# Later row groups' preparation two attention steps later in every engine's queue: a graph attention and mixture-of-experts kernel

## The chip, the cores and the metric

The kernel runs on one core of a Trainium2 chip. The metric is the device time of one execution in microseconds. The engines are TensorE (PE; its weight loads are PEld), VectorE (DVE), ScalarE (ACT), GpSimd (POOL) and SyncE (SP), which issues transfers. Each has a queue of its own that it works off in order, and they meet only at semaphores.

## The reference

4096 rows x of 128 features, a sparse 4096 x 4096 adjacency matrix (entries 0 or 1), one attention head, then eight experts of which each row takes two:

```python
h = layernorm(x)
Wh = h @ W_w + W_b
e = leaky_relu((Wh @ a1)[:, None] + (Wh @ a2)[None, :], 0.2)
x = x + softmax(where(adj > 0, e, -9e15), axis=1) @ Wh
g = layernorm(x)
top, idx = top_k(g @ Wg.T + bg, 2)
p = softmax(top)
x = x + sum over the two experts e in idx of p_e * (relu(g @ W1[e].T + b1[e]) @ W2[e].T + b2[e])
```

## The kernel before, in words

**Rows and steps.** Of the 4096 rows, partition p holds rows 32p to 32p + 31; column u of that layout is a source tile of 128 rows (TILES = 32), and four neighbouring tiles are a row group i (GROUPS = 8). The attention runs in five stages over the target rows (8, 8, 8, 6 and 2 tiles wide), each over all 32 source tiles: 160 attention steps n. The change concerns the first stage, steps 0 to 31, where the source rows are prepared as they are needed.

**One attention step.** SP loads the mask as int32, a mask tile for two steps at a time; ACT turns it into bf16 (`edges`, L1321, into G_all); DVE weighs a tile (`weigh`, L948: prob from G_all, a row vector s_bc and the column E_col of this source tile); PE multiplies it with the source rows (`attend`, L1548, acc<-prob,Wh, two multiplications of 512 columns, four records in the trace). prob has six buffers, G_all four. DVE's loop runs four steps ahead of PE's (LB), ACT's mask tiles six (LG), SP's loads twelve (LS).

**Preparing a row group i.** Sums of a row (`stats`, DVE, L867 to L872) give its variance; POOL raises it to -1/2 (`pow_group`, L693 to L701); ACT normalises into Wh (`normalise`, L1286); PE transposes (`transposes`, L1499); ACT copies the result (`keep_hT`, L1295); PE projects it (`project`, L1509, into pj; for groups 2 and 3 `project_s`, L1518, as well); ACT makes two columns of it, w_col and E_col (`keep_E`, L1302 and L1303, and `keep_s`, L1313, for groups 2 and 3); DVE rescales the group's Wh with w_col (`keep_Wh`, L887). Weighing of step 4i waits for E_col of group i, and PE's step 4i for its rescaled Wh. Groups 0 and 1 are prepared ahead of the loop.

**What sets the order.** Each engine has a function `main` that walks n and writes at each n what belongs there; `group_at(n, part)` says which group has its turn in that place, every fourth step:

```python
def group_at(n, part, first=2):
    i, r = divmod(n - part, 4)
    return i + 2 if r == 0 and first <= i + 2 < GROUPS else None
```

**What else stands in these queues.** The experts' first-layer weights are brought in during the stage: ACT issues the loads (`load_expert`, L1337 to L1339), POOL subtracts a row (`shift_weights`, L707), ACT writes the high part (`high_weights`, L1331), DVE the low part (`low_weights`, L1005), for expert 0 at n = 8, 10, 12 and for expert 1 at n = 14, 16, 18, expert 2 at n = 20, 22, 24. At n = 18 DVE writes Wx (L1234, L1235), at n = 20 PE turns it (`gate_weights`, L1694, L1695), at n = 26 DVE makes the gate's terms (L1226 to L1229), and at n = 28 PE needs them (`gate_columns`, L1700). s_bc of the second stage is capped at n = 24 (L933). Behind the first stage, attention steps, sending of rows to their experts and the experts' multiplications are interleaved by counts of the same n.

Of the kernel before, what the change touches and what calls it, by code (L numbers as in the profile page):

```python
# [5 lines left out]
def build(nc, x, adjT, W, Wb, a, WgT, bg, wcat, wlast, b2, out):  # L6
# [119 lines left out]
    with ctx:  # L126
# [319 lines left out]
# [4 lines that stand above are left out]
# [398 lines left out]
        def _(dve):  # L848
# [81 lines left out]
            def group_row(g):  # L930
                dve.wait_ge(s_sbc, (AT[g] + WB[g] + GT - 1) // GT)
                c = c_bc[:, P * AT[g]:P * (AT[g] + WB[g])]
                nc.vector.tensor_scalar(c, c, 1.0, None, ALU.min).then_inc(s_cg, 1)  # L933
# [271 lines left out]
            def main(general):  # L1205
                for n in range(-LB, NS):
# [1 line left out]
                    if m < STEPS and (m or general):  # L1208
                        (weigh_general if general else weigh)(m)
                    if not general:  # L1210
                        i = group_at(n, -7, 4)
                        if i is not None:
                            stats(i)
                        i = 1 if n == -1 else group_at(n, 3)
                        if i is not None:
                            keep_Wh(i, False)
                        if n >= 0 and n % TILES == TILES - 8 and n // TILES + 1 < SG:
                            group_row(n // TILES + 1)
# [42 lines left out]
            with dve.If(fast != 0):  # L1261
                group_row(0)
                weigh(0)
                keep_Wh(0, False)
                stats(3)
                main(False)
            with dve.Else():
                links[0] = before
# [13 lines left out]
        def _(act):  # L1282
# [123 lines left out]
            def main(general):  # L1406
                ahead = LB if general else LG
                for n in range(-ahead, NS):
# [3 lines left out]
                    if m < STEPS and general:  # L1412
                        raise_tile(m)
                    if not general:
                        i = group_at(n, -1)
                        if i is not None:
                            normalise(i)
                        i = group_at(n, 2)
                        if i is not None:
                            keep_hT(i)  # L1420
                        if n == -1:
                            keep_E(1)
                        i = group_at(n, 3)
                        if i is not None:
                            keep_E(i)
                            if i < GT:
                                keep_s(i, general)
                        i = row_at(n)
                        if i is not None:
                            keep_s(i, general)  # L1430
# [59 lines left out]
        def _(pe):  # L1490
# [211 lines left out]
            def main(general):  # L1702
                for n in range(NS):
                    if n == 20:
                        gate_weights()
                    if n == 28:
                        pe.wait_ge(s_xg, 1)
                        gate_columns()
                    if not general:
                        i = group_at(n, 1)  # L1710
                        if i is not None:
                            transposes(i)
                        if n == 1:
                            project(1)
                        i = group_at(n, 3)
                        if i is not None:
                            project(i)
                            if i < GT:
                                project_s(i)
                        i = row_at(n)  # L1720
                        if i is not None:
                            project_s(i, True)
                    if n >= STEPS:
                        tail_beat(TAIL + n - STEPS)
                    if n < STEPS:
                        attend(n)
                    for part in parts_of(n):
                        finish(*part)
# [53 lines left out]
```

## Time and profile before

| | us |
|---|---|
| three runs | 450.41, 452.68, 457.28 (median 452.68) |
| the profiled execution, whole | 449.83 |
| its span on the core | 448.1 |
| PE busy in the span | 396.3 (88%) |
| DVE, ACT, POOL busy | 294.0, 263.9, 200.6 |

The span is the time from the first to the last instruction in the profile; the execution's own time has 1.7 us more around it. Starts in the profile are counted from the start of the span. A row of the timeline merges neighbouring instructions of a kind; its time runs from the first start to the last end, and ends overlap the next start a little, so the step from one row's start to the next is the better measure of pace.

### The profile page before, as it was taken

What the parts mean: (1) busy time and instruction counts of PE and PEld (TensorE: products, weight loads), DVE (VectorE), ACT (ScalarE), POOL (GpSimd) and SP (SyncE); (2) the same over time, 40 slices, a digit from 0 to 9 for tenths busy, and PEclk for the clock granted to TensorE, in tenths of its full rate; (3) what the DMA queues carried; (4) which work ended last, traced back from release to release, by engine and by line L of the source; (5) the groups of instructions that cost most, each with busy time, mean ns of one, the idle gap of its engine ahead of it and who ended that gap; (6) DMA issues with size and microseconds to landing.
All of it is one profiled execution on the core that took longest, in us unless ns stands there. A gap on an engine that the chain in (4) does not pass through costs nothing.

```text
span 448.1 us, 8397 instructions
## 1 busy us (share of the span) xinstructions
PE 396.3 (88%) x2434; PEld 262.8 (59%) x2434; DVE 294.0 (66%) x806; ACT 263.9 (59%) x451; POOL 200.6 (45%) x247
## 2 busy tenths in 40 slices
PE   2799999999999999989999999898789798899960
PEld 2355555354444444434666777686679788888850
DVE  5889879988999796999878831887105800111162
ACT  1688888387677757924679545373346345555630
POOL 3373411100415752066431877766666644444460
PEclk9899999999999999999999999999899979999995
DMA  6999898869698997985879663664656545565784
GB/s 212 362 419 348 324 318 290 369 241 384 266 314 317 337 414 251 324 303 170 302 236 378 214 194 129 215 198 155 215 182 218 186 164 163 174 216 183 240 329 144
DMA packets 45324, 116.46 MB, mean 260 GB/s; under 512 B 7485, under 2 KB 19266, under 8 KB 38614
## 3 DMA queue, kind: packets, MB, share of 16 engines
q1 hardware_dynamic: 37494, 101.07, 63.5%
q0 software_dynamic: 4320, 8.47, 5.6%
q10 hardware_dynamic: 3456, 6.29, 4.4%
q8 instruction: 23, 0.38, 0.4%
q14 instruction: 31, 0.25, 0.2%
HBM read 84.57 MB, written 13.07 MB: 218 GB/s over the span
## 4 chain that ended last, share of the span: by engine, by line
PE 66%; issue 9%; DMA 6%; DVE 6%; ACT 6%; SPq 3%; another core or an unknown queue 2%; POOL 1%; ACTq 0%; POOLq 0%; DVEq 0%
PE acc L1548 36%; PE acc L1650 11%; DVE prob L948 3%; PE hps L1634 3%; PE hps L1632 3%; PE hps L1633 3%; ACT G_all L1321 3%; PE yt L1650 3%; DMA adj<-adjT 3%; PE yt L1593 2%; PE pj L1509 1%; DMA xbuf<-xr,slot 1%; DMA adj<-ybuf 1%; PE pj L1669 1%
## 5 line engine op out<-in xcount | busy, mean ns | idle before, releaser
L1548 PE MATMUL acc<-prob,Wh 128*128 128x512 f32 (+1 forms) x576 | 237.7, 553 | 6.7 <-DVE Wh L887 3.1
L948 DVE SCALAR_TENSOR_TENSOR prob<-s_bc,E_col,G_all 128x1024 f32<-128x1024 f32 (+2 forms) x160 | 172.0, 1105 | 31.8 <-PE acc L1548 20.0
L1548 PEld LDWEIGHTS acc<-prob,Wh 128*128 128x128 f32 x576 | 104.5, 192 | 101.7 <-issue 88.2
L1321 ACT ACTIVATE G_all<-adj 128x2048 bf16<-128x2048 int32 (+1 forms) x67 | 118.9, 1800 | 19.0 <-DVE prob L948 10.3
L799 POOL DMA_INDIRECT ybuf<-wst,dest x71 | 73.0, 1028 | 70.0 <-ACT wst L1404 41.5
L783 POOL DMA_INDIRECT xbuf<-xr,slot x64 | 72.2, 1128 | 56.5 <-DVE slot L1105 19.6
L1650 PE MATMUL acc<-wall,prob 128*128 x368 | 54.1, 289 | 4.5 <-issue 4.5
L1650 PEld LDWEIGHTS acc<-wall,prob 128*128 128x128 f32 x368 | 46.5, 196 | 6.1 <-issue 5.3
L1192 DVE COPY share<-slab 128x1 f32<-128x1 f32 x45 | 6.9, 157 | 62.2 <-DMA slab<-xbuf 41.0
L1394 ACT ACTIVATE prob<-hps 128x512 f32<-128x512 f32 x46 | 28.0, 608 | 31.5 <-PE hps L1634 19.3
L1394 ACT ACTIVATE wst<-hps 128x512 f32<-128x512 f32 x25 | 14.9, 598 | 22.8 <-remote 17.1
L1650 PE MATMUL yt<-wall,wst 128*128 x192 | 27.3, 286 | 0.0
L707 POOL TENSOR_TENSOR wst<-wst,wlb 127x512 f32<-127x512 f32 x8 | 12.0, 1508 | 33.9 <-DMA wlb<-wlast 33.9
L1650 PEld LDWEIGHTS yt<-wall,wst 128*128 128x128 f32 x192 | 23.7, 194 | 4.1 <-issue 2.6
L693 POOL TENSOR_TENSOR scratch<-scratch,mhalf 128x4 f32<-128x4 f32 x8 | 13.4, 1675 | 26.9 <-DVE scratch L872 26.9
L1633 PE MATMUL hps<-prob,s_bc 128*128 128x128 f16 x124 | 23.0, 222 | 1.0 <-issue 1.0
L1632 PE MATMUL hps<-prob,s_bc 128*128 128x128 f16 x124 | 22.9, 222 | 0.8 <-issue 0.8
L1634 PE MATMUL hps<-prob,s_bc 128*128 128x128 f16 x124 | 23.1, 222 | 0.0
L1404 ACT ACTIVATE wst<-acc,share 128x128 f32<-128x128 f32 x45 | 16.6, 372 | 10.8 <-PE acc L1650 6.9
L1593 PE MATMUL yt<-ident,slab 128*128 128x128 f16 x142 | 19.7, 220 | 3.5 <-issue 2.0
L765 POOL TENSOR_TENSOR rstd<-ve,mhalf 128x8 f32<-128x8 f32 x3 | 5.5, 1824 | 34.4 <-DVE ve L1050 34.4
L1389 ACT ACTIVATE prob<-yt 128x256 f16<-128x256 f16 x45 | 17.6, 392 | 5.2 <-PE yt L1593 3.2
(237 smaller groups left out, 543.8 us busy)
## 6 DMA issues: line engine op xcount, KB each, us to landing
adj<-adjT SPq DMA_DIRECT2D x52, 1024.0 KB
adj<-adjT SPq DMA_DIRECT2D x16, 768.0 KB
s_bc<-wall SPq DMA_DIRECT2D x47, 256.0 KB
wlb<-wall SPq DMA_DIRECT2D x24, 256.0 KB
slab<-xbuf SPq DMA_DIRECT2D x71, 65.0 KB
adj<-ybuf SPq DMA_DIRECT2D x6, 512.0 KB
xs<-x SPq DMA_DIRECT2D x8, 256.0 KB, 10.6
wst<-wcat ACTq DMA_DIRECT2D x8, 256.0 KB, 4.6
```

What stands on the lines that cost most here:

```text
L783: nc.gpsimd.indirect_dma_start(xbuf[:, :], bass.IndirectOffsetOnAxis(ap=slot[:, w, b:b + 1].bitcast(u32), axis=0), xr[:, w, b, :], None).t ...
L799: nc.gpsimd.indirect_dma_start(ybuf[:, :], bass.IndirectOffsetOnAxis(ap=dest[:, t:t + 1].bitcast(u32), axis=0), ysb[t % YR][:, :], None, b ...
L948: nc.vector.scalar_tensor_tensor(prob[n % PR][:, 0:w], c_bc[:, P * AT[g]:P * AT[g] + w], E_col[:, u:u + 1], G[m % GR][:, k * w:(k + 1) * w ...
L1321: nc.scalar.activation(G[m % GR][:, 0:w], adj_sb[m % AR][:, 0:w], ACT.Relu).then_inc(s_G, 1)
L1389: nc.scalar.activation(xT_of(t), tps_of(t), ACT.Copy).then_inc(s_xT, 1)
L1394: nc.scalar.activation(hid_of(t), hps[t % 2][:, :], ACT.Relu).then_inc(s_hh, 1)
L1548: last = nc.tensor.matmul(bank[:, 0:k * P], Wh[:, u, :], prob[n % PR][:, b * P:(b + k) * P], start=(u == 0), stop=(u == TILES - 1), skip_g ...
L1593: last = nc.tensor.transpose(tps_of(t)[:, h * P:(h + 1) * P], x16[:, h * P:(h + 1) * P], ident16[:, :])
L1632: nc.tensor.matmul(dst, whi, xhi, start=(k == 0), stop=False, skip_group_check=True)
L1633: nc.tensor.matmul(dst, whi, xlo, start=False, stop=False, skip_group_check=True)
L1634: last = nc.tensor.matmul(dst, wlo, xhi, start=False, stop=True, skip_group_check=True)
L1650: last = nc.tensor.matmul(yps, hid_of(t)[:, j * P:(j + 1) * P], weights(t, UW + 2 * j * P, 2 * P).bitcast(fp32), start=False, stop=(j == K ...
```

## The change

The calls for the later groups (2 and up; sums from 3 up) are written two steps later in all queues that have them: sums of group i at n = 4i - 13 instead of 4i - 15 (group 3, which was ahead of the loop, now at n = -1), normalise at 4i - 7 instead of 4i - 9, transposes at 4i - 5 instead of 4i - 7, copy at 4i - 4 instead of 4i - 6, projection, columns and rescaling at 4i - 3 instead of 4i - 5. POOL's queue, the mask tiles, the weighings, the experts' weights and the gate's terms keep their places.

```diff
--- before.py
+++ after.py
@@ -1208,10 +1208,10 @@
                     if m < STEPS and (m or general):
                         (weigh_general if general else weigh)(m)
                     if not general:
-                        i = group_at(n, -7, 4)
+                        i = group_at(n, -5, 3)
                         if i is not None:
                             stats(i)
-                        i = 1 if n == -1 else group_at(n, 3)
+                        i = 1 if n == -1 else group_at(n, 5)
                         if i is not None:
                             keep_Wh(i, False)
                         if n >= 0 and n % TILES == TILES - 8 and n // TILES + 1 < SG:
@@ -1262,7 +1262,6 @@
                 group_row(0)
                 weigh(0)
                 keep_Wh(0, False)
-                stats(3)
                 main(False)
             with dve.Else():
                 links[0] = before
@@ -1412,15 +1411,15 @@
                     if m < STEPS and general:
                         raise_tile(m)
                     if not general:
-                        i = group_at(n, -1)
+                        i = group_at(n, 1)
                         if i is not None:
                             normalise(i)
-                        i = group_at(n, 2)
+                        i = group_at(n, 4)
                         if i is not None:
                             keep_hT(i)
                         if n == -1:
                             keep_E(1)
-                        i = group_at(n, 3)
+                        i = group_at(n, 5)
                         if i is not None:
                             keep_E(i)
                             if i < GT:
@@ -1707,12 +1706,12 @@
                         pe.wait_ge(s_xg, 1)
                         gate_columns()
                     if not general:
-                        i = group_at(n, 1)
+                        i = group_at(n, 3)
                         if i is not None:
                             transposes(i)
                         if n == 1:
                             project(1)
-                        i = group_at(n, 3)
+                        i = group_at(n, 5)
                         if i is not None:
                             project(i)
                             if i < GT:
```

One line less stands ahead of ACT's and PE's code, so its line numbers are one lower afterwards (L1331 becomes L1330). In the rows below, [waits ...] names the semaphores of an instruction.

ACT between the columns of group 4 and those of group 5, before: G_all is a mask tile, hps1 the transposed group 5, wall<-wst1 the high part of expert 1.

```order
L1321 ACTIVATE G_all<-adj1 128x2048 [waits s_P,s_adj1]
L1295 ACTIVATE wall,hsum8<-hps1 128x512 [waits s_t0]
L1321 ACTIVATE G_all<-adj2 128x2048 [waits s_P,s_adj2]
L1286 ACTIVATE Wh<-xs,nm0,scratch 128x127 [waits s_rstd]
L1286 ACTIVATE Wh<-xs,nm0,scratch 128x127 x3
L1302 ACTIVATE w_col<-pj,bD,dsc 128x4 [waits s_wh]
L1303 ACTIVATE E_col<-pj,bE 128x4
L1321 ACTIVATE G_all<-adj3 128x2048 [waits s_P,s_adj3]
L1331 ACTIVATE wall<-wst1 128x4x128 [waits s_wsc]
```

The same place of ACT in the changed kernel:

```order
L1294 ACTIVATE wall,hsum8<-hps1 128x512 [waits s_t0]
L1320 ACTIVATE G_all<-adj3 128x2048 [waits s_P,s_adj3]
L1330 ACTIVATE wall<-wst1 128x4x128 [waits s_wsc]
L1336 DMA wst0<-wcat 128x512 [waits s_wlo]
L1337 DMA wlb0<-wlast 128x512
L1338 DMA wall<-wcat 128x512
L1285 ACTIVATE Wh<-xs,nm0,scratch 128x127 [waits s_rstd]
L1285 ACTIVATE Wh<-xs,nm0,scratch 128x127 x3
L1301 ACTIVATE w_col<-pj,bD,dsc 128x4 [waits s_wh]
L1302 ACTIVATE E_col<-pj,bE 128x4
```

The high part of expert 1, which waits for POOL (s_wsc), stood behind normalise(6) and the columns of group 5; now it and three issues stand ahead of them.

DVE from the rescaling of group 4 to the sums of group 7, before (scratch holds the sums, prob4 and prob5 are steps 16 and 17, wall<-wst0 the low part of expert 0):

```order
L887 TENSOR_TENSOR Wh<-Wh,w_col 128x512 [waits s_ED]
L948 SCALAR_TENSOR_TENSOR prob4<-s_bc,E_col,G_all 128x1024 [waits s_at,s_G,s_ED]
L1005 SCALAR_TENSOR_TENSOR wall<-wst0,wall 128x4x128 [waits s_whi]
L948 SCALAR_TENSOR_TENSOR prob5<-s_bc,E_col,G_all 128x1024 [waits s_at,s_G]
L867 BN_STATS scratch<-xs 128x6 [waits s_xin7]
L867 BN_STATS scratch<-xs 128x6 x3
L870 BN_AGGR scratch<-scratch 128x2 [waits s_pl]
L870 BN_AGGR scratch<-scratch 128x2 x3
L872 TENSOR_SCALAR scratch<-scratch 128x4 [waits s_pl]
```

In the changed kernel:

```order
L948 SCALAR_TENSOR_TENSOR prob4<-s_bc,E_col,G_all 128x1024 [waits s_at,s_G,s_ED]
L1005 SCALAR_TENSOR_TENSOR wall<-wst0,wall 128x4x128 [waits s_whi]
L948 SCALAR_TENSOR_TENSOR prob5<-s_bc,E_col,G_all 128x1024 [waits s_at,s_G]
L887 TENSOR_TENSOR Wh<-Wh,w_col 128x512 [waits s_ED]
L948 SCALAR_TENSOR_TENSOR prob0<-s_bc,E_col,G_all 128x1024 [waits s_at,s_G]
L948 SCALAR_TENSOR_TENSOR prob1<-s_bc,E_col,G_all 128x1024 [waits s_at,s_G]
L867 BN_STATS scratch<-xs 128x6 [waits s_xin7]
L867 BN_STATS scratch<-xs 128x6 x3
L870 BN_AGGR scratch<-scratch 128x2 [waits s_pl]
L870 BN_AGGR scratch<-scratch 128x2 x3
L872 TENSOR_SCALAR scratch<-scratch 128x4 [waits s_pl]
```

The rescaling of group 4 moved from ahead of step 16 to behind step 17, and the sums of group 7 from behind step 17 to behind step 19.

PE around the turning of Wx (L1694, s_wx), before: hps0<-ident,Wh are the transposes of group 6, pj the projection of group 5, prob1 step 19 and prob2 step 20.

```order
L1499 MATMUL hps0<-ident,Wh 128x128 [waits s_hT,s_xh]
L1499 MATMUL hps0<-ident,Wh 128x128 x3
L1548 MATMUL acc0<-prob5,Wh 128x512 [waits s_P]
L1548 MATMUL acc1<-prob5,Wh 128x512
L1548 MATMUL acc0<-prob0,Wh 128x512 [waits s_P]
L1548 MATMUL acc1<-prob0,Wh 128x512
L1509 MATMUL pj<-wag,wall 128x9 [waits s_whs,s_hT]
L1509 MATMUL pj<-wag,wall 128x9 x3
L1548 MATMUL acc0<-prob1,Wh 128x512 [waits s_P]
L1548 MATMUL acc1<-prob1,Wh 128x512
L1694 MATMUL yt<-ident,Wx 128x128 [waits s_wx]
L1695 MATMUL yt<-WgT_sb,ones 128x8
```

In the changed kernel:

```order
L1508 MATMUL pj<-wag,wall 128x9 [waits s_whs,s_hT]
L1508 MATMUL pj<-wag,wall 128x9 x3
L1547 MATMUL acc0<-prob5,Wh 128x512 [waits s_P]
L1547 MATMUL acc1<-prob5,Wh 128x512
L1547 MATMUL acc0<-prob0,Wh 128x512 [waits s_P]
L1547 MATMUL acc1<-prob0,Wh 128x512
L1498 MATMUL hps0<-ident,Wh 128x128 [waits s_hT,s_xh]
L1498 MATMUL hps0<-ident,Wh 128x128 x3
L1547 MATMUL acc0<-prob1,Wh 128x512 [waits s_P]
L1547 MATMUL acc1<-prob1,Wh 128x512
L1693 MATMUL yt<-ident,Wx 128x128 [waits s_wx]
L1694 MATMUL yt<-WgT_sb,ones 128x8
```

The projection of group 5 stands ahead of step 17 instead of step 19, and the transposes of group 6 directly ahead of step 19 instead of step 17; L1694 keeps its place ahead of step 20.

## Rows read from the trace of the kernel before

**Rows 1.** Page, engines over the span: busy us, share, instructions.

```profile
PE 396.3 (88%) x2434; PEld 262.8 (59%) x2434; DVE 294.0 (66%) x806; ACT 263.9 (59%) x451; POOL 200.6 (45%) x247
```

**Rows 2.** Page, chain that ended last, shares of the span.

```profile
PE 66%; issue 9%; DMA 6%; DVE 6%; ACT 6%; SPq 3%; another core or an unknown queue 2%; POOL 1%; ACTq 0%; POOLq 0%; DVEq 0%
```

**Rows 3.** Timeline of PE: start us, us, instruction, count, [idle before <-releaser].

```profile
19.86 3.39 PE L1548 MATMUL acc<-prob,Wh 128*128 128x512 f32 x4 [3.07 <-DVE Wh L887]
23.83 0.66 PE L1499 MATMUL hps<-ident,Wh 128*128 128x128 f32 x4 [0.58 <-ACT Wh L1286]
...
42.89 0.60 PE L1499 MATMUL hps<-ident,Wh 128*128 128x128 f32 x4
43.33 3.60 PE L1548 MATMUL acc<-prob,Wh 128*128 128x512 f32 x8
46.76 0.95 PE L1509 MATMUL pj<-wag,wall 128*128 128x9 f32 x8
47.57 3.68 PE L1548 MATMUL acc<-prob,Wh 128*128 128x512 f32 x8
...
65.77 0.27 PE L1694 MATMUL yt<-ident,Wx 128*128 128x128 f32 x1
...
82.13 0.39 PE L1700 MATMUL yt<-Wgc,scratch 128*128 128x9 f32 x2 [0.80 <-DVE xnT L1229]
...
202.06 10.23 PE L1548 MATMUL acc<-prob,Wh 128*128 128x512 f32 x23 [2.57 <-DVE prob L948]
```

**Rows 4.** Timeline of DVE, first attention stage, same columns.

```profile
32.65 0.69 DVE L887 TENSOR_TENSOR Wh<-Wh,w_col 128x512 f32<-128x512 f32 x1
33.26 2.47 DVE L948 SCALAR_TENSOR_TENSOR prob<-s_bc,E_col,G_all 128x1024 f32<-128x1024 f32 x2
35.65 0.86 DVE L867 BATCH_NORM_STATS2 scratch<-xs 128x6 f32<-128x128 f32 x4
...
37.04 2.48 DVE L948 SCALAR_TENSOR_TENSOR prob<-s_bc,E_col,G_all 128x1024 f32<-128x1024 f32 x2
...
53.42 0.17 DVE L872 TENSOR_SCALAR scratch<-scratch 128x4 f32<-128x4 f32 x1
...
62.26 0.28 DVE L1235 TENSOR_TENSOR Wx<-Wx,wlast_bc 127x128 f32<-127x128 f32 x1
...
77.93 3.49 DVE L948 SCALAR_TENSOR_TENSOR prob<-s_bc,E_col,G_all 128x1024 f32<-128x1024 f32 x2
```

**Rows 5.** Timeline of ACT, first attention stage.

```profile
20.33 1.91 ACT L1321 ACTIVATE G_all<-adj 128x2048 bf16<-128x2048 int32 x1 [1.19 <-DMA adj<-adjT]
...
54.11 1.63 ACT L1286 ACTIVATE Wh<-xs,nm,scratch 128x127 f32<-128x127 f32 x4
55.96 0.35 ACT L1302 ACTIVATE w_col<-pj,bD,dsc 128x4 f32<-128x4 f32 x1 [0.21 <-PE pj L1509]
56.21 0.26 ACT L1303 ACTIVATE E_col<-pj,bE 128x4 f32<-128x4 f32 x1
...
58.16 0.63 ACT L1331 ACTIVATE wall<-wst 128x512 f16<-128x512 f32 x1
```

**Rows 6.** Timeline of POOL, first attention stage.

```profile
16.04 1.40 POOL L693 TENSOR_TENSOR scratch<-scratch,mhalf 128x4 f32<-128x4 f32 x1 [3.31 <-DVE scratch L872]
...
53.66 1.99 POOL L693 TENSOR_TENSOR scratch<-scratch,mhalf 128x4 f32<-128x4 f32 x1 [6.01 <-DVE scratch L872]
...
56.27 1.27 POOL L707 TENSOR_TENSOR wst<-wst,wlb 127x512 f32<-127x512 f32 x1
...
78.87 1.47 POOL L707 TENSOR_TENSOR wst<-wst,wlb 127x512 f32<-127x512 f32 x1 [10.44 <-DMA wlb<-wlast]
```

**Rows 7.** Windows: stretch, us, busy of each engine, granted clock (PEclk), DMA.

```profile
core 0: us, PE busy (x) PEld busy (x) DVE busy (x) ACT busy (x) POOL busy (x), PEclk, DMA share, GB/s
16.80:19.30 2.50, 0.00 (x0) 0.00 (x0) 2.03 (x3) 2.31 (x3) 1.04 (x3) 1.00 0.98 383
19.30:22.60 3.30, 2.74 (x4) 1.17 (x4) 3.23 (x12) 2.27 (x3) 1.36 (x1) 0.51 1.03 408
82.00:434.00 352.00, 327.20 (x2208) 226.09 (x2208) 221.36 (x642) 205.73 (x367) 170.04 (x182) 0.99 0.71 248
```

## The prediction

> **What bounds the kernel now.** I read the page's table of engines first: TensorE (PE) is busy for 88% of the span [rows 1], and the chain that ended last is two thirds PE [rows 2]. Then the timeline of PE over the first attention stage, since only that stage holds instructions that the diff moves. PE has one gap of 0.58 us ahead of the transposes of group 2, then no pause at all up to one of 0.80 us at 82.13, where it waits for L1229 of VectorE [rows 3]. So in this stretch everything that delays a PE instruction lengthens the kernel, and everything that only fills another engine's slack does not. The units, taken from one start to the next [rows 3]: two attention steps take 43.33 to 46.76, 3.43 us, so a step is 1.72; the projection of a group is 46.76 to 47.57, 0.81; the four transposes of a group 0.44. On VectorE (DVE) [rows 4] a weighing step is 2.39 / 2 = 1.20, rescaling a group of Wh 0.61 (32.65 to 33.26), the sums of a group 1.39 (35.65 to 37.04), L1235 0.28; for the low part of an expert and for L933, elementwise passes of about that size, I use the rescaling's 0.6. On ScalarE (ACT) [rows 5] normalising a group is 1.6 us, the pair w_col and E_col 0.5 (55.96 to 56.47), a mask tile 1.8 to 1.9 (1.91 less the overlap of neighbours), the high part of an expert 0.6. PE's demand per group is 4 x 1.72 + 0.81 + 0.44 = 8.1 us, DVE's 4 x 1.20 + 0.61 + 1.39 = 6.8: PE sets the pace, with DVE close behind.
>
> **What the change does to the start.** No instruction is added or removed. Sums of group 3 leave the place ahead of weighing step 1, so that steps 1 to 3 are weighed 1.39 us earlier; PE doesn't need them earlier, since it is busy with step 0 to 23.25. PE can now project group 1 at once and do steps 1 and 2, but group 2 is now normalised behind the scaling columns of group 1 and one more mask tile: projection 23.25 to 24.06, columns 24.1 to 24.6, mask tile to 26.4, normalisation to 27.9, where PE has been free since 24.06 + 3.43 = 27.5. A gap of 0.4 takes the place of one of 0.58: **-0.2 us**, with bounds -0.6 (no gap) and +1.0 (the mask tile late by 1.19 us for its load, as the one of 20.33 was [rows 5]).
>
> **Steady groups.** Let T be the end of PE's step 12. Each chain of a group (sums, power, normalisation, transposes, copy, projection, columns, rescaling) moves as a whole, so its inner distances stay. What shrinks is the distance to the step that needs the group: the columns of group i are made behind step 4i-4 instead of 4i-6. From the end of that step: projection 0.81, columns 0.5, two weighings 2.4, rescaling 0.61, 4.3 us in all and 4.9 with an expert's low part between; PE has 0.81 + 3 x 1.72 + 0.44 = 6.4 to do before it needs them. That costs **nothing**, and the cover is PE's own work; 1.5 us is left of it.
>
> **The fixed instructions between.** This is where I expect the loss. GpSimd's queue isn't moved: pow of group 7 stands ahead of the subtraction for expert 1 (L707), and ACT's high part of expert 1 (L1331) is not moved either, but now stands ahead of normalise(6) and the columns of group 5, which had been ahead of it. Before, the sums of group 7 ended at 53.59 [rows 4], the subtraction at 57.54 [rows 6], and ACT took L1331 at 58.16 [rows 5]: 0.6 us of slack and nothing urgent behind. Now, from T: projection 4 and its columns, T+1.3; steps 16 and 17 weighed with an expert's low part between and the rescaling, 3.6, T+4.9; two more weighings, T+7.3; sums of group 7, T+8.7. From there to the end of L707 it was 3.95 us; with DVE idle, as it will be, the earlier pow of 16.04 took 1.40 instead of 1.99 [rows 6], which gives 3.2. So T+11.9 to 12.6. Then L1331 0.55 and normalise(6) 1.6: T+14.1 to 14.8. PE arrives at transposes(6) at T + 0.81 + 3.43 + 0.44 + 3.43 + 0.81 + 3.43 = T+12.35. **PE waits 1.8 to 2.4 us; I take 2.1.** Queued behind the waiting L1331 on ACT: three DMA issues, normalise(6), the columns of group 5, and for these waits DVE's weighing of step 20.
>
> **The second wait.** Those columns end 0.5 after normalise(6). DVE then weighs 20 and 21, rescales group 5, weighs 22, makes the low part of expert 1, and does L1234 and L1235: 2.4 + 0.61 + 1.2 + 0.6 + 0.26 = 5.07. PE has the transposes and step 19, 0.44 + 1.72 = 2.16, and then stands at L1694, which wants L1235 and is in front of step 20. 0.5 + 5.07 - 2.16 = 3.4: **+3.4 us**. Before, L1235 ended at 62.54 [rows 4] and PE came to L1694 only at 65.77, without a wait [rows 3].
>
> **The third wait.** In front of step 28 PE wants L1229. From the end of projection 7: columns 0.5, weighing 28 1.2, L933 0.61, low part of expert 2 0.60, two short ones 0.27, weighing 29 1.2, rescaling of group 7 0.61 (new in this place), weighing 30 1.2, L1226 to L1229 0.65 (81.42 to the release of PE at about 82.1): 6.85, against three PE steps, 5.15. That is 1.7. In the trace, weighings 29 and 30 took 3.49 us instead of 2.4 while GpSimd ran L707 at 78.87 [rows 4, 6]. L707 waits for weights whose loading is issued at an unmoved place, so it moves about as PE does and I let it fall into this stretch again: 1.7 + 1.0 = 2.7, less the 0.80 there before, **+1.9 us** (0.9 without the overlap).
>
> **The sum.** -0.2 + 2.1 + 3.4 + 1.9 = +7.2 us. I expect it to reach the end, because after 82 us the largest idle of PE that another engine's work ended is 2.57 us, at 202.06 [rows 3], and all later work is released by counts of the same steps. The profiled execution took 449.83; the runs shown are 450.41, 452.68 and 457.28. The middle of the four is 451.5, and 451.5 + 7.2 = **458.7 us**. From the median of the three it would be 459.9, from the profiled one 457.0.
>
> **TensorE's clock.** PE stood idle for 3.07 us up to 19.86; the granted clock was 1.00 up to 19.3 and then 0.50 (1.2 GHz) through 22.6, so that the four records of step 0 took 3.39 us instead of 1.72 [rows 3, 7]. The idle of 2.57 at 202.06 was followed by 23 records in 10.23 us, 0.44 each, full clock [rows 3]. The second wait, 3.4 us, is longer than either. In that first case the low level held for 3.3 us, 0.6 of them idle; if it falls in the second wait, with 0.9 of its 3.3 us idle and 2.4 in work at half speed, 1.2 us are lost, and at most the 1.7 that step 0 lost.
>
> The Trainium skill, TensorE: Matmul & The Clock Gate, Part 1 and its section on HAM oscillation, has the array's clock drop to half after idle and come back only after sustained work, and so speaks against a change that makes PE wait. The fall at 19.3 agrees. By that rule the sum would be 8.4 to 8.9 instead of 7.2.
>
> **Rivals.** *The clock falls* in the second wait: 7.2 + 1.2 to 1.7 = 8.4 to 8.9, some 460.2 us. For it: the row at 19.3. Against it: the waits come in a stage where PE is otherwise full. With the longer pow (+0.4) and a slow spell in the first wait too, it is over 10: 461.7.
>
> *GpSimd is not late.* If L707 for expert 1 ended before ACT is through with the mask tile in front of L1331, the first two waits vanish and only the start and the third are left: -0.2 + 1.9 = 1.7, 453.2 us. It decides at T+7.1 (the transposes of group 5 end at T+4.7, copy 0.6, mask tile 1.8), 5 us before the time that I work out. For it: nothing but an error in the chain, such as sums of group 7 that need not wait for the columns of group 4. Against it: the order of both queues.
>
> *Swallowed later*, the one that ends not slower: From 82 to 434 us PE is idle for 24.8 us in all (352 less 327.2) [rows 7]. If those were set by transfers that run by their own clock (the mask loads, the scatter of rows), a PE that is 7.2 us late would find them landed and wait less: 7.2 back, 451.5 us. It decides when at least 7 of those 24.8 us are freed. Against it: the loads are issued when buffers of the same steps come free, and scatters by the count of steps done.
>
> **How the numbers follow.** Chances: the forecast 0.42; clock falls once 0.20; over 10 us of loss 0.13; GpSimd not late 0.16; swallowed 0.09. A measurement of this kernel can tell about 2%, 9 us, from no change: that is 460.5. Above it lie the 0.13, half of the clock case and a little of the forecast's own spread, 0.26; faster by 2% takes something that I don't see, 0.02; within 2% 0.72. The range leaves out the end of the heavy case and a part of the swallowed one: 452 to 465, which takes in the bounds of the start, the third wait without overlap, and the base (449.8 to 452.7).
>
> **What would show it.** After: L1331 for expert 1 waiting some 5 us for L707, released by GpSimd; PE idle before L1498 (transposes of group 6) about 2 us, before L1693 about 3.4, before L1699 about 2.7; the gate columns at about 89 us instead of 82.13; sums of group 7 ending 5 us later than 53.6. Wrong if PE runs through these three places, or if the 82.13 point moves and the end does not.

## The result, and the profile after

The changed kernel takes 463.93 us (median of 4 runs, 460.02 to 465.28), the kernel before 454.06 (4 runs, 450.41 to 457.28): 1.0256 times as long, 95% interval 1.0197 to 1.0315. Two later measurements of the same pair gave 1.0246 (1.0193 to 1.0300) and 1.0217 (1.0173 to 1.0261). Some executions, whatever the kernel, fall in a slower state, up to 819.91 and 1042.21 us in two of the experiments below, and the ratios leave those out. So the change loses 10 to 12 us where I had forecast 7.2: right in sign, and too small.

PE is busy for longer, and its share of the chain that ended last has gone down in favour of DVE. The page's lines, to be set against [rows 1, 2]:

```profile
PE 403.5 (87%) x2434; PEld 266.7 (58%) x2434; DVE 293.8 (64%) x806; ACT 265.3 (57%) x451; POOL 197.2 (43%) x247
...
PE 61%; DVE 13%; issue 7%; ACT 6%; DMA 4%; another core or an unknown queue 3%; SPq 3%; POOL 1%; ACTq 0%; DVEq 0%; POOLq 0%
```

The timeline of PE in the changed kernel, to be set against [rows 3]:

```profile
19.27 3.75 PE L1547 MATMUL acc<-prob,Wh 128*128 128x512 f32 x4 [3.07 <-DVE Wh L887]
22.81 1.72 PE L1508 MATMUL pj<-wag,xnT 128*128 128x9 f32 x8
24.38 5.69 PE L1547 MATMUL acc<-prob,Wh 128*128 128x512 f32 x8
29.91 0.60 PE L1498 MATMUL hps<-ident,Wh 128*128 128x128 f32 x4
...
66.86 0.66 PE L1498 MATMUL hps<-ident,Wh 128*128 128x128 f32 x4 [2.27 <-ACT Wh L1285]
67.35 1.88 PE L1547 MATMUL acc<-prob,Wh 128*128 128x512 f32 x4
73.50 0.48 PE L1693 MATMUL yt<-ident,Wx 128*128 128x128 f32 x1 [4.26 <-DVE Wx L1235]
...
74.05 3.76 PE L1547 MATMUL acc<-prob,Wh 128*128 128x512 f32 x4
77.61 1.72 PE L1508 MATMUL pj<-wag,wall 128*128 128x9 f32 x8
79.17 5.61 PE L1547 MATMUL acc<-prob,Wh 128*128 128x512 f32 x8
...
96.49 0.39 PE L1699 MATMUL yt<-Wgc,scratch 128*128 128x9 f32 x2 [1.79 <-DVE xnT L1229]
```

The three waits that the prediction named are there, at the places named: 2.27 us at the transposes of group 6 (forecast 2.1), 4.26 at L1693 (forecast 3.4), 1.79 at the gate columns (forecast 2.7, and 0.80 before). The wait of 0.58 at the start is gone. The gate columns come at 96.49 instead of 82.13, 14.4 us later, and the span is 13.7 longer. (One group number above the prediction is wrong: the projection that stood ahead of step 19 is that of group 6, here at 77.61 ahead of step 21; that of group 5 came from ahead of step 15.) But three rows are also simply slow: from the start of step 20 at 74.05 to the next row are 3.56 us where a step is 1.72, the projection behind it takes 1.56 instead of 0.81, steps 21 and 22 take 5.45 instead of 3.43. Together that is 1.84 + 0.75 + 2.02 = 4.6 us which no wait shows. The start has the same: step 0, the projection and steps 1 and 2 run from 19.27 to 29.91, 10.6 us for work that takes 6.0 at the pace of [rows 3].

What holds the first wait, on ACT, GpSimd and DVE, to be set against [rows 4 to 6]:

```profile
57.45 1.90 ACT L1320 ACTIVATE G_all<-adj 128x2048 bf16<-128x2048 int32 x1
63.81 0.63 ACT L1330 ACTIVATE wall<-wst 128x512 f16<-128x512 f32 x1 [4.46 <-POOL wst L707]
...
65.17 1.64 ACT L1285 ACTIVATE Wh<-xs,nm,scratch 128x127 f32<-128x127 f32 x4 [0.73 <-issue]
...
66.95 0.24 ACT L1302 ACTIVATE E_col<-pj,bE 128x4 f32<-128x4 f32 x1
```

```profile
60.99 1.01 POOL L693 TENSOR_TENSOR scratch<-scratch,mhalf 128x4 f32<-128x4 f32 x1 [7.61 <-DVE scratch L872]
...
62.51 1.26 POOL L707 TENSOR_TENSOR wst<-wst,wlb 127x512 f32<-127x512 f32 x1
68.44 1.27 POOL L707 TENSOR_TENSOR wst<-wst,wlb 127x512 f32<-127x512 f32 x1 [4.66 <-DMA wlb<-wlast]
83.69 1.80 POOL L707 TENSOR_TENSOR wst<-wst,wlb 127x512 f32<-127x512 f32 x1 [13.98 <-DMA wlb<-wlast]
```

```profile
60.74 0.17 DVE L872 TENSOR_SCALAR scratch<-scratch 128x4 f32<-128x4 f32 x1
67.23 3.55 DVE L948 SCALAR_TENSOR_TENSOR prob<-s_bc,E_col,G_all 128x1024 f32<-128x1024 f32 x2 [6.32 <-ACT E_col L1302]
...
73.17 0.28 DVE L1235 TENSOR_TENSOR Wx<-Wx,wlast_bc 127x128 f32<-127x128 f32 x1
...
84.27 3.49 DVE L948 SCALAR_TENSOR_TENSOR prob<-s_bc,E_col,G_all 128x1024 f32<-128x1024 f32 x2
```

Read from GpSimd back: the sums of group 7 end at 60.91 (53.59 before), the power takes 60.99 to 62.56, the subtraction for expert 1 to 63.77, and only then can ACT write the high part, for which it has stood 4.46 us; three issues of loads (0.73 us), normalise(6) and the columns of group 5 come behind it, and DVE has been idle 6.32 us for them. The two weighings at 67.23 then take 3.55 instead of 2.4 us, while GpSimd runs its next subtraction (68.44, for expert 2). This overlap I had left out of the second wait. The one that I had put into the third wait is another, with the subtraction for expert 3 (78.87 before): it now runs at 83.69 beside the weighings at 84.27, which take 3.49 us, and PE waits for nothing there.

The granted clock (PEclk) in windows of the changed kernel, to be set against [rows 7]:

```profile
core 0: us, PE busy (x) PEld busy (x) DVE busy (x) ACT busy (x) POOL busy (x), PEclk, DMA share, GB/s
18.70:27.90 9.20, 8.63 (x16) 4.57 (x17) 8.17 (x16) 5.24 (x7) 3.51 (x4) 0.50 1.02 420
62.00:72.60 10.60, 4.96 (x15) 1.87 (x13) 5.37 (x5) 8.00 (x13) 2.88 (x5) 1.00 0.66 214
72.60:82.90 10.30, 9.40 (x20) 5.27 (x21) 4.97 (x7) 5.42 (x9) 0.00 (x0) 0.51 0.52 176
```

It is at 2.4 GHz through the first wait and most of the second, up to 72.6, then at 1.2 GHz for 10.3 us; and at 1.2 GHz for 9.2 us and a little more behind the idle ahead of step 0, where the profile of before had 3.3.

### The profile page after: what moved, and what is told of

It reads as the page before. It is cut to its first block, busy times and chain, and to the rows that moved or that the text cites. A ratio compares the mean times of both kernels' runs of the same rounds, so it can differ in the third digit from the quotient of the medians.

```text
span 461.8 us, 8397 instructions
## 1 busy us (share of the span) xinstructions
PE 403.5 (87%) x2434; PEld 266.7 (58%) x2434; DVE 293.8 (64%) x806; ACT 265.3 (57%) x451; POOL 197.2 (43%) x247
## 4 chain that ended last, share of the span: by engine, by line
PE 61%; DVE 13%; issue 7%; ACT 6%; DMA 4%; another core or an unknown queue 3%; SPq 3%; POOL 1%; ACTq 0%; DVEq 0%; POOLq 0%
PE acc L1547 33%; PE acc L1649 10%; DVE prob L948 6%; PE hps L1633 3%; ACT G_all L1320 3%; PE hps L1631 3%; PE hps L1632 3%; PE yt L1649 2%; PE yt L1592 1%; PE pj L1508 1%; DMA xbuf<-xr,slot 1%; SPq L541 1%; DMA adj<-ybuf 1%; PE pj L1668 1%
## 5 line engine op out<-in xcount | busy, mean ns | idle before, releaser
L1547 PE MATMUL acc<-prob,Wh 128*128 128x512 f32 (+1 forms) x576 | 244.0, 565 | 7.2 <-DVE Wh L887 3.1
L1547 PEld LDWEIGHTS acc<-prob,Wh 128*128 128x128 f32 x576 | 106.8, 196 | 104.5 <-issue 90.1
L1320 ACT ACTIVATE G_all<-adj 128x2048 bf16<-128x2048 int32 (+1 forms) x67 | 119.0, 1800 | 20.3 <-DVE prob L948 10.3
L1393 ACT ACTIVATE prob<-hps 128x512 f32<-128x512 f32 x46 | 27.9, 606 | 30.8 <-remote 15.1
L1649 PE MATMUL yt<-wall,wst 128*128 x192 | 27.9, 290 | 0.0
L693 POOL TENSOR_TENSOR scratch<-scratch,mhalf 128x4 f32<-128x4 f32 x8 | 8.3, 1041 | 36.2 <-DVE scratch L872 36.1
L1592 PEld LDWEIGHTS yt<-ident,slab 128*128 128x128 f16 x142 | 13.7, 100 | 14.1 <-issue 9.0
## 6 DMA issues: line engine op xcount, KB each, us to landing
xs<-x SPq DMA_DIRECT2D x8, 256.0 KB, 10.6
```

Source lines behind the costliest of these rows:

```text
L1320: nc.scalar.activation(G[m % GR][:, 0:w], adj_sb[m % AR][:, 0:w], ACT.Relu).then_inc(s_G, 1)
L1393: nc.scalar.activation(hid_of(t), hps[t % 2][:, :], ACT.Relu).then_inc(s_hh, 1)
L1547: last = nc.tensor.matmul(bank[:, 0:k * P], Wh[:, u, :], prob[n % PR][:, b * P:(b + k) * P], start=(u == 0), stop=(u == TILES - 1), skip_g ...
L1592: last = nc.tensor.transpose(tps_of(t)[:, h * P:(h + 1) * P], x16[:, h * P:(h + 1) * P], ident16[:, :])
L1649: last = nc.tensor.matmul(yps, hid_of(t)[:, j * P:(j + 1) * P], weights(t, UW + 2 * j * P, 2 * P).bitcast(fp32), start=False, stop=(j == K ...
```

## The experiments

The diffs below are cut to what matters. "Gate columns" is the start of L1700 (or its like) in the profile; up to there the kernels differ, behind it they all run the same code.

**Which groups lose.** Groups 2 and 3 moved alone, and groups 4 to 7 moved alone; `at2` gives group_at's answer two steps later for the groups in the list.

```diff
+            for late in (0, 2):
+                i = group_at(n - late, part, first)
+                if i is not None and (i in (2, 3)) == (late == 2):
+                    return i
-                        i = group_at(n, 3)
+                        i = at2(n, 3)
...
-                stats(3)
```

> The kernel before with only groups 2 and 3 moved two steps later (sums of group 3 behind weighing 3); groups 4 to 7 in their old places. Theory (the loss at the start is a longer slow spell of TensorE's clock behind step 0, not a wait): no wait of PE at the transposes of group 6 nor at L1694, about 0.8 us before the gate columns as before, and a total between +0 and +3 us against before, depending on how long the 1.2 GHz spell behind step 0 lasts (3.4 us before, about 9 us in the changed kernel). Rival (the order of groups 2 and 3 itself costs): PE idle of over 1 us ahead of the transposes of group 2 or of step 8, and the loss is there even with a short slow spell.

Measured: 1.0011 (0.9956 to 1.0066), gate columns at 84.43, one wait of 0.8 us for a rescaled group at the projection of group 4, none at group 6 or at the gate. With `(4, 5, 6, 7)` in the list, and the sums of group 3 left where they were:

> The kernel before with only groups 4 to 7 moved two steps later; the start is as before. Theory (the loss comes from the fixed instructions between the moved ones): waits of PE of 2.3 us at the transposes of group 6, 4.3 at the gate weights, a slow spell of the clock behind the second wait that costs 4 to 5 us, 1.8 in place of 0.8 at the gate columns: +11 to +12 us against before. Rival (the loss comes from the start): under +3.

Measured: 1.0288 (1.0182 to 1.0394), +13 us, gate columns at 95.93. So the loss belongs to groups 4 to 7. Rows of PE in this kernel:

```profile
69.30 0.72 PE L1507 MATMUL hps<-ident,Wh 128*128 128x128 f32 x4 [2.28 <-ACT Wh L1294]
69.82 3.56 PE L1556 MATMUL acc<-prob,Wh 128*128 128x512 f32 x4
75.94 0.33 PE L1702 MATMUL yt<-ident,Wx 128*128 128x128 f32 x1 [2.57 <-DVE Wx L1243]
```

The same first wait to 0.01 us. Here the clock had fallen by the end of that first wait already (0.52 from 69.6 to 73.0): step 19 was slow, which shortened the second wait from 4.26 to 2.57 and so cost nothing, and step 20 was slow again (3.2). Behind the waits the low clock cost this profile only 1.7 us (from step 20 to the end of the projection 4.30 us instead of 2.6); its start, 13.4 us at 1.2 GHz, makes up for it.

**The subtraction ahead of the power of group 7**, in the changed kernel:

```diff
                         if not general:
                             i = group_at(n, -7, 4)
+                            if i == 7:
+                                shift_weights(1)
                             if i is not None:
                                 pow_group(i)
...
-                    if e is not None:
+                    if e is not None and (general or e != 1):
                         shift_weights(e)
```

> The changed kernel with one thing moved: on GpSimd the subtraction for expert 1 (L707) stands ahead of the power of group 7. Theory: ScalarE's high part of expert 1 doesn't wait any more, the first wait of PE (2.3 us) vanishes, the second shrinks from 4.3 to about 1 us, the clock doesn't fall there; 8 to 10 us faster than the changed kernel, +2 to +4 against before. Rival (DVE or ScalarE are simply too full for the later places): the columns of group 5 come as late as before this edit, and the time stays within 2 us of the changed kernel.

Measured: 1.0057 (1.0008 to 1.0106), gate columns at 85.97. All waits of PE from 24 to 98 us in it (engine, line, released by: us, times, longest):

```profile
PE yt L1701 <- DVE xnT L1231: 1.8, 1, 1.8
PE yt L1695 <- DVE Wx L1237: 1.4, 1, 1.4
```

The first wait is gone, the second 1.36, the third as before the edit; no slow stretch between 62 and 90 us. Some 9 us of the loss, the low clock behind the second wait included, hang on one instruction of 1.26 us that stood behind the wrong wait.

**And L1234, L1235 earlier** (`n == 18` becomes `n == 14`), on top of it:

```diff
-                    if n == 18:
+                    if n == 14:
                         dve.wait_ge(s_wf, 32)
```

> The changed kernel with the subtraction for expert 1 ahead of the power of group 7, and in addition VectorE's L1234 and L1235 written at n = 14 instead of 18, so that the gate weights wait for nothing late. Theory (what is left of the second wait, 1.36 us, was DVE's chain behind the columns of group 5): that wait vanishes, the one at the gate columns stays at 1.8, and the time is 1 to 1.5 us below the kernel with the subtraction alone moved, so about +1 us against before. Rival (the DVE chain is the bound, and a wait removed at the gate weights comes back at the rescaled Wh of group 5 in front of step 20): PE idle of about 1 us in front of step 20 and no gain.

Measured: 1.0082 (1.0042 to 1.0123), gate columns at 86.50. The theory's gain did not come (the interval overlaps the one above), though the wait at the gate weights and any in front of step 20 are gone: the wait at the gate columns grew from 1.79 to 2.98. Its cause in the rows of DVE and GpSimd:

```profile
80.06 1.87 DVE L935 TENSOR_SCALAR s_bc<-s_bc 128x1024 f32<-128x1024 f32 x1
81.85 0.67 DVE L1007 SCALAR_TENSOR_TENSOR wall<-wst,wall 128x512 f16<-128x512 f32 x1
```

```profile
79.64 1.63 POOL L707 TENSOR_TENSOR wst<-wst,wlb 127x512 f32<-127x512 f32 x1 [11.69 <-DMA wlb<-wlast]
```

GpSimd's subtraction for the next expert, which waits for a load, now fell onto DVE's chain to the gate's terms (L1229, here L1231), where L935 took 1.87 instead of the 0.69 in the kernel above. So 1.36 us were taken away in one place and 1.2 came back in the next, where DVE's chain is the bound.

**The clock.** Extra multiplications of constants keep PE busy in a wait; `fill(k)` is k times a 128 x 128 product of ones into a bank that is written over later, and shows as 2k records. First 16 of them ahead of the gate weights' wait:

```diff
             def gate_weights():
 
+                fill(16)
                 pe.wait_ge(s_wx, 1)
```

> The changed kernel with 16 extra 128 x 128 multiplications of constants (3.5 us of work) put in PE's queue ahead of its wait at the gate weights; they write a bank that is overwritten after. The waits on the other engines stay. Theory (4 to 5 us of the loss are half speed behind the second wait): the granted clock stays at 2.4 GHz through 66 to 85 us and the kernel is 4 to 5 us faster than the changed one, +8 against before. Rival (the waits alone make the loss, and a slow spell is hidden by the waits behind it): the time stays within 1 us of the changed kernel, or rises by what the extra work is late.

Measured: 1.0208 (1.0126 to 1.0290), median 460.69. The clock stayed at 1.00 from 62 to 91 us and the gate columns came at 91.62, 4.9 us before those of the changed kernel. The profiled run as a whole was 465.04, slower than the other four (460.19 to 461.91); from its gate columns to the end it took 371.7 us, the longest of all profiles here. So I filled both waits, with the changed kernel beside it on one chip:

```diff
+                        if i == 6:
+                            fill(9)
                         if i is not None:
                             transposes(i)
```

> The changed kernel with constants multiplied in both waits: 9 extra multiplications (1.9 us) ahead of the transposes of group 6 and 16 (3.5 us) ahead of the gate weights. Theory (slow spells behind the waits cost 3 to 5 us on top of them): no spell between 62 and 90 us, the three waits' ends where they were, 3 to 5 us below the changed kernel of the same call, 1.4 to 1.8% above before. Rival (no cost of the clock in the time as measured): equal to the changed kernel within 1 us.

> The changed kernel beside the one with both waits filled, on the same chip in five rounds, so that the two can be compared through before: 2.2 to 2.8% above before by either theory; what tells is the distance to the filled one (3 to 5 us by the theory of the clock, under 1 by the rival).

Measured: 1.0155 (1.0113 to 1.0196) with the waits filled, median 460.86; 1.0217 (1.0173 to 1.0261) for the changed kernel, median 463.36. The filled kernel, window and timeline of PE:

```profile
core 0: us, PE busy (x) PEld busy (x) DVE busy (x) ACT busy (x) POOL busy (x), PEclk, DMA share, GB/s
62.00:90.00 28.00, 25.58 (x116) 15.62 (x114) 21.54 (x28) 22.41 (x30) 3.61 (x7) 1.00 0.74 249
```

```profile
62.95 2.17 PE L1693 MATMUL yt<-ones 128*128 128x128 f32 x18
65.38 0.66 PE L1498 MATMUL hps<-ident,Wh 128*128 128x128 f32 x4 [0.27 <-ACT Wh L1285]
...
67.59 3.73 PE L1693 MATMUL yt<-ones 128*128 128x128 f32 x32
71.97 0.33 PE L1699 MATMUL yt<-ident,Wx 128*128 128x128 f32 x1 [0.65 <-DVE Wx L1235]
...
90.28 0.39 PE L1705 MATMUL yt<-Wgc,scratch 128*128 128x9 f32 x2 [1.80 <-DVE xnT L1229]
90.53 14.29 PE L1547 MATMUL acc<-prob,Wh 128*128 128x512 f32 x28
```

The row behind the gate columns in the changed kernel's first profile, to be set against the last of these:

```profile
96.73 12.60 PE L1547 MATMUL acc<-prob,Wh 128*128 128x512 f32 x28
```

Normalise(6) releases at 65.38 instead of 66.86 and L1235 at 71.97 instead of 73.50, both 1.5 us earlier, which is what a shorter slow stretch behind step 0 gave this profile (6.7 us against 10.3). PE does no more useful work than before, and by the estimates the kernel is 0.6% faster, 2.5 us by the medians. The two intervals overlap from 1.0173 to 1.0196, and 2.5 us is less than the 3 to 5 that I expected. In the profiles the filled kernel is 6.2 us ahead at the gate columns; less the 1.5 of the start, that leaves 4.7 for the clock between 62 and 90 us, where it is 1.00 throughout. A part may be lost again directly behind: in both kernels with filled waits the clock falls behind the third wait, which was not filled, and the 28 records there take 14.29 us, as against 12.60 in two of the changed kernel's three profiles (14.28 in the third, the one beside the filled kernel). How much of the 4.7 us reaches the end is told by the times alone, 2.5 us.

**Is the slow stretch at the start part of the change?** The kernel before once more:

> The kernel before once more, for a second profile of its start. Theory (the length of the slow spell behind step 0 is chance and no part of the change: 3.4 us in the one profile of before, about 10 in every profile of a kernel with the changed start, but over 10 as well in the one whose start was left as before): a spell of about 10 us is as likely here as a short one. Rival (the old start gives the short one): 3.4 us again.

Measured: eight runs, 446.19 to 456.85, median 455.33, beside 452.8 for 17 other runs of the same kernel. The recorded ratio, 0.9896 (0.9839 to 0.9953), rests on two of the eight. So one and the same kernel can differ by 0.6 to 1% here, and a difference of 0.6%, such as that of the filled waits, rests on the profiles as much as on the times. The window of the slow stretch, and two rows of PE:

```profile
core 0: us, PE busy (x) PEld busy (x) DVE busy (x) ACT busy (x) POOL busy (x), PEclk, DMA share, GB/s
18.20:31.60 13.40, 11.56 (x23) 5.89 (x24) 10.35 (x27) 8.87 (x14) 7.03 (x26) 0.50 0.99 398
```

```profile
23.79 1.11 PE L1499 MATMUL hps<-ident,Wh 128*128 128x128 f32 x4 [0.84 <-ACT Wh L1286]
...
85.17 0.39 PE L1700 MATMUL yt<-Wgc,scratch 128*128 128x9 f32 x2
```

13.4 us at 1.2 GHz in the unchanged kernel, and gate columns at 85.17. So the length of this stretch is no part of the change. The first profile of before, with its 82.13, had a short one, 3 us better than the second; its 449.83 us are also 3 us under the medians of before (452.6 to 454.1). Which of the two is the usual one, two profiles can't say; groups 4 to 7 alone, with the same start, had 13.4 us as well. The changed kernel's second profile:

> The changed kernel once more, for its time beside before on this chip and for a second profile. Theory (the waits are fixed by the queues, the slow spells vary in length with where they happen to fall): the same three waits within 0.3 us, and one or two slow spells whose lengths differ from the first profile's 10 and 10 us; +9 to +14 us against before. Rival (the spells are fixed by the program too): the same spells within 1 us.

Measured: 1.0246, the same three waits (2.28, 4.21, 1.79), slow stretches of 10.4 and 10.2 us, gate columns at 95.76. That the lengths would differ did not come out here, and in this the rival was right; over the profiles of all kernels they differ.

**Filling the start of the kernel before**, 12 multiplications ahead of step 0:

```diff
             with pe.If(fast != 0):
+                fill(12)
                 main(False)
```

> The kernel before with 12 extra 128 x 128 multiplications of constants (2.6 us) in PE's queue between its prologue and step 0, where it is idle for 3.07 us; they write a bank that is overwritten later. Theory (the low spells that follow the 3 us idle, 3.4 us long in the profile of before and about 10 in five others, are set off by that idle): no spell behind step 0, step 0 takes 1.7 us instead of 3.4, and the kernel is 2 to 5 us faster than before. Rival (the spell is due to the light work of the prologue as a whole, or its cost is hidden by waits for masks and columns at the start): the clock falls all the same, or PE idles for as long as it saves; within 1 us of before.

Measured: 0.9987 (0.9949 to 1.0025). Rows of PE:

```profile
16.45 2.92 PE L1694 MATMUL yt<-ones 128*128 128x128 f32 x24
19.67 1.96 PE L1548 MATMUL acc<-prob,Wh 128*128 128x512 f32 x4 [0.29 <-issue]
24.16 0.66 PE L1499 MATMUL hps<-ident,Wh 128*128 128x128 f32 x4 [2.54 <-ACT Wh L1286]
```

Step 0 runs at full speed, and PE then waits 2.54 us at the transposes of group 2, which ACT's mask tile and normalisation hold; the clock fell behind that, from 25.9 to 29.2. The rival held: PE waits about as long as step 0 saves. With the gate columns one step later in addition (`n == 28` becomes `29`):

> The kernel before with the 12 extra multiplications, and PE's gate columns at n = 29 instead of 28. Theory: the wait of 0.8 us at the gate columns vanishes as well, 0.5 to 0.8 us below the kernel with the extra multiplications alone; 3 to 5 us faster than before. Rival: since step 28 itself waits for its weighing on the late DVE, the wait only moves there and nothing is gained over the extra multiplications.

Measured: 1.0017 (0.9976 to 1.0058); PE doesn't wait at the gate columns any more (its wait at the transposes of group 2 was 1.71 us in this profile) and no slow stretch came before 90 us, yet nothing is gained that this measurement can tell. None of these beats the kernel before.

**One step later instead of two**:

```diff
-                        i = group_at(n, -5, 3)
+                        i = group_at(n, -6, 3)
...
-                        i = group_at(n, 1)
+                        i = group_at(n, 0)
                         if i is not None:
                             normalise(i)
```

and so on for each moved call, in the changed kernel.

> The same groups moved one step later instead of two (sums of group i at n = 4i - 14, normalisation 4i - 8, projection, columns and rescaling 4i - 4). On ScalarE normalise(6) and the columns of group 5 are then still ahead of the high part of expert 1. Theory (the loss is that crossing and what follows from it): no wait at the transposes of group 6 nor at the gate weights, 1 to 2 us at the gate columns, within 2 us of before. Rival (each step later costs its share of slack): about half of the changed kernel's loss, +5 us.

Measured: 1.0103 (1.0060 to 1.0145), +4.8 us. The number is the rival's, the mechanism neither's. A row of PE and four of ACT:

```profile
71.09 1.88 PE L1508 MATMUL pj<-wag,wall 128*128 128x9 f32 x8 [3.77 <-ACT wall L1294]
```

```profile
64.50 0.63 ACT L1330 ACTIVATE wall<-wst 128x512 f16<-128x512 f32 x1 [2.48 <-POOL wst L707]
...
65.35 0.81 ACTq L1338 DMA_DIRECT2D wall<-wcat  x1
66.26 1.91 ACT L1320 ACTIVATE G_all<-adj 128x2048 bf16<-128x2048 int32 x1 [1.13 <-DVE wall L1005]
...
70.22 0.60 ACT L1294 ACTIVATE wall<-hps 128x512 f32<-128x512 f32 x1
```

normalise(6) is indeed ahead of the high part of expert 1, and no wait is at the transposes. But the sums of group 7 still come later, the high part waits 2.48 us for the subtraction, and the mask tile stands behind it and behind ACT's three issues of loads, which end at 66.16 (the row puts its 1.13 us to DVE, but this tile waits only for its load and for weighings long done). The copy of group 6 stands behind all this and two small copies (L1435 and L1437, 2.1 us): PE waits 3.77 us at its projection, and the clock falls for 6.8 us. I had followed the one crossing that I knew, and not the next instruction behind the same wait.

## Why the prediction was right in kind and wrong in size

The step that failed is the clock of TensorE, which the sum takes at nothing. The runs showed 4.6 us for it up to the gate columns and 2.5 to 3.2 us in the whole time. Here is the span up to the gate columns, in the terms of the prediction. The changed kernel's 96.49 are 14.4 us behind the first profile of before (82.13, with a short slow stretch at the start) and 11.3 behind the second (85.17, with a long one); the times give 10 to 12.

- **The start, -0.2.** The wait of 0.58 (0.84 in the second profile) at the transposes of group 2 is gone, so about -0.6; that there is no wait at all is partly the slow clock, since PE came to these transposes only at 29.91, 1.5 us after ACT had done (28.41, forecast 27.9). Groups 2 and 3 moved alone cost 0.5 us by the estimate of the ratio, with zero inside its interval. Right, and nearly nothing. The slow stretch there moves the profiles more: for equal work done, the changed kernel begins step 17 1.6 us behind the first profile of before and 2.2 ahead of the second.
- **Steady groups, nothing.** Right: PE has no wait between 19.27 and 64.5.
- **First wait, 2.1.** 2.27, by the mechanism named; in both further profiles 2.28 and 2.27. The subtraction's place was its whole cause, as moving it showed. That the number is so near is in part luck: from the end of the sums to the end of the subtraction it was 2.9 us instead of the 3.2 to 3.95 assumed, and the three issues on ACT, which the prediction lists but does not price, took 0.73. The faster power that I assumed for an idle DVE held: 1.01 us against 1.99 [rows 6]. The Trainium skill says of this, in GPSIMD Engine Reference, section Key points, that GpSimd shares its SBUF interfaces with VectorE; the rows agree, with L693 at 1.01 us beside an idle DVE and 1.99 beside weighings.
- **Second wait, 3.4.** 4.26, of it 1.1 from the overlap of weighings 20 and 21 with GpSimd's subtraction for expert 2, which the prediction left out. **Third wait, +1.9.** +1.0 (1.79 less 0.80): 1.7 was right for the chain, and the overlap with the subtraction for expert 3 was not there. The two together are 5.3 forecast and 5.3 measured, by luck: the two errors of 0.9 us cancel.
- **TensorE's clock, 0 in the sum.** This is the term that failed. I put the fall of the clock down as a rival of 1.2 to 1.7 us with a chance of 0.20, and made the forecast without it, though the longest wait that my rows showed without a fall was 2.57 us and the second wait was to be 3.4. It fell in all three profiles of the changed kernel, and in that of groups 4 to 7 alone. Its price up to the gate columns was 4.6 us in the profile and 4.7 to 4.9 by filling the waits, but 1.7 in groups 4 to 7 alone, where a part was hidden in the second wait; by the medians of whole times it is 2.5 on one chip (460.86 against 463.36), 3.2 across two measurements (460.69 against 463.93). I had sized it from the one slow stretch that the profile showed, 3.3 us long; the stretches behind idle PE were 3.4 to 13.4 us long in the further profiles, and the one in question 10.3. With the clock held in both waits the loss is 8.1 us by the medians (460.86 less 452.8), near the 7.2 of the waits.
- **The sum.** With the start's slow stretch left out, -0.6 + 2.3 + 4.3 + 1.0 + 4.6 = 11.6, against 7.2. The waits alone come to 7.0. With that stretch in, and 0.3 us for the turning of Wx at the low clock, the terms add up to 1.6 + 2.3 + 4.3 + 1.0 + 4.9 = 14.1 of the 14.4 us against the first profile of before, and, with no wait at the gate columns in the second, to -2.2 + 2.3 + 4.3 + 1.8 + 4.9 = 11.1 of the 11.3 against that.
- **The base.** I took 451.5 us; the medians of 17 to 29 runs of before are 452.6 to 453.3. The forecast 458.7 was too low by that as well, by 1 to 2 us.
- **Reaching the end.** From the gate columns to the end of the span took 366.0 and 369.9 us in the two profiles of before, and 365.3, 368.6 and 369.5 in the three of the changed kernel: no sign that anything is swallowed or added, within a scatter of 4 us. Over all kernels here it is 363.1 to 371.7, which is more than the 3 us of the start.

The measured 463.93 lies near the upper end of the range (452 to 465), which I had drawn for other reasons: I gave 0.72 to a difference within 2%, and all three measurements are above that. The rival *GpSimd is not late* fell with the first wait; *swallowed later* with the tail. The heavy case (two spells, over 10 us, 461.7, chance 0.13) was the nearest of all in number; its second spell isn't there in the changed kernel, one spell was as dear as that alone.

## What to carry to other kernels

When a chain is moved as a block through several queues, list for each queue what stays: the damage is done by the unmoved instruction that now stands in front of a moved one and waits for an engine whose own queue wasn't moved, and then by the next ones behind the same wait. A forced wait of 3 to 4 us of TensorE may have to be priced at more than its length: here waits of 7.0 us in all cost 10 to 12. A price taken from one row of a thing that varies, such as a slow stretch of the clock, is one draw and no bound, and a second profile of the same kernel is the cheapest way to see that.

## What the runs showed of the hardware that was not expected

- Slow stretches of the clock behind the idle ahead of step 0 were 3.4 us in one profile of before and 13.4 in the other, with the same instructions and the same 3.07 us of idle; 6.7 to 10.4 us in the kernels with the changed start. Within them PE was not idle for long: it was busy 8.63 of 9.20 us in the changed kernel and 11.56 of 13.40 in the second profile of before.
- A wait of 2.28 us at full clock was followed by a slow step in one kernel (groups 4 to 7 alone), and one of 2.27 us was not in the changed kernel, where the clock fell only in the second wait, at 72.6.
- GpSimd's 127 x 512 subtraction (1.26 us beside an idle DVE) stretches the DVE weighings beside it by about 1.1 us, nearly its own length, and an operation of DVE with one input too (L935 1.87 instead of 0.69). It goes both ways: in the kernel of one step later the same subtraction took 2.31 us at 62.16, beside weighings.
